# The last stage's value bias: added by a transfer from DRAM instead of by GpSimd, and a third hidden weight tile

## The reference, cut to what matters

```
def _L3_conv_ref(x, in_proj_weight, in_proj_bias, hid_proj_weight, hid_proj_bias, out_proj_weight, out_proj_bias):
    qkv = in_proj_weight[None] * x[:, None, :, :, :, None] + in_proj_bias[None]
    q = softplus(qkv[:, 0].reshape(n, -1, a))
    k = softplus(qkv[:, 1].reshape(n, -1, a))
    v = qkv[:, 2].reshape(n, -1, a)
    s = cumsum(k[:, :, :, None] * v[:, :, None, :], axis=1)
    z = cumsum(k, axis=1)
    y = einsum('nsi,nsij->nsj', q, s) / einsum('nsi,nsi->ns', q, z)[:, :, None]
    y = concatenate([ones_like(y[:, :1]), y[:, :-1]], axis=1)
    y = sum(hid_proj_weight[None] * y[:, None], axis=-1) + hid_proj_bias[None]
    y = sum(out_proj_weight[None] * tanh(y), axis=1) + out_proj_bias[None]
```

## Time and profile before

| what | us |
|---|---|
| median of three runs (3159.19, 3159.97, 3163.45) | 3159.97 |
| the profiled execution | 3161.46 |
| its span in the trace | 3159.7 |
| busy in it: VectorE | 1936.3 |
| GpSimd | 1770.5 |
| TensorE | 1537.9 |
| ScalarE | 863.4 |
| last stage, from about 2196 to the end | 964 |

### The profile page before, as it was taken

How to read it: one execution, slowest core, us unless ns; L and a number is a source line. 1 busy time by engine, 2 the same in 40 slices (tenths; PEclk the granted TensorE clock), 3 DMA queues, 4 the chain that set the end, 5 groups by cost and what they waited for, 6 DMA issues and landing times. The chain is left out here.

```text
span 3159.7 us, 31596 instructions
## 1 busy us (share of the span) xinstructions
PE 1537.9 (49%) x11604; PEld 875.4 (28%) x11604; DVE 1936.3 (61%) x1751; ACT 863.4 (27%) x1126; POOL 1770.5 (56%) x1350
## 2 busy tenths in 40 slices
PE   3656551323222222223222220054688888898998
PEld 2545420101000100001000010043255555555555
DVE  4222145555555545555455554467899999999995
ACT  2111151111111111111111110053545545455451
POOL 2000017777777777777777777605455465564652
PEclk9787865555555555555555555568799999999999
DMA  9999864655555445555555545233031231322312
GB/s 365 404 429 429 366 172 133 160 146 141 133 148 149 134 133 139 153 138 137 137 141 152 135 133 136 85 127 84 7 121 64 83 106 66 117 69 76 113 64 94
DMA packets 337029, 483.27 MB, mean 153 GB/s; under 512 B 185920, under 2 KB 277076, under 8 KB 319184
## 3 DMA queue, kind: packets, MB, share of 16 engines
q1 hardware_dynamic: 278256, 329.84, 30.8%
q0 software_dynamic: 58720, 152.72, 17.3%
HBM read 396.89 MB, written 85.45 MB: 153 GB/s over the span
## 5 line engine op out<-in xcount | busy, mean ns | idle before, releaser
L435 POOL DMA_INDIRECT gath<-table,idx x1152 | 1212.1, 1052 | 436.8 <-issue 375.3
L610 DVE TENSOR_TENSOR gath<-gath,p_stat 128x2304 f32<-128x2304 f32 x128 | 326.9, 2554 | 749.8 <-DMA gath<-table,idx 672.6
L647 PE MATMUL p_z<-wz,pairs 128*128 128x384 f32 x384 | 266.8, 827 | 456.0 <-issue 452.3
L493 ACT ACTIVATE zt<-p_z 128x384 f32<-128x384 f32 x192 | 93.5, 491 | 984.6 <-remote 627.2
L647 PEld LDWEIGHTS p_z<-wz,pairs 128*128 128x128 f32 x384 | 100.9, 302 | 610.6 <-issue 600.2
L637 PE MATMUL p_conv<-sides,wconv 128*128 128x512 f32 x64 | 66.2, 1138 | 398.7 <-issue 314.6
L1039 POOL TENSOR_TENSOR gated<-gated,outw_early 128x512 f32<-128x512 f32 x64 | 133.0, 2078 | 216.4 <-ACT gated L1100 216.4
L1269 PE MATMUL p_state<-xt,tri_early 128*128 128x512 f32 x512 | 235.2, 602 | 28.5 <-DVE prod L1155 28.5
L1155 DVE TENSOR_TENSOR prod<-p_state,query 128x2048 f32<-128x2048 f32 x80 | 182.0, 2275 | 54.4 <-PE p_state L1279 53.8
L289 PE MATMUL acc<-ring,win_a 128*32 128x128 f32 x3072 | 135.1, 342 | 145.2 <-DMA ring<-in_w 126.6
L655 PE MATMUL p_y<-ident,yt 128*128 128x128 f32 x64 | 17.8, 432 | 382.3 <-DVE yt L618 382.3
(11 more groups left out here) (242 smaller groups left out, 3084.4 us busy)
## 6 DMA issues: line engine op xcount, KB each, us to landing
ring<-in_w SPq DMA_DIRECT2D x64, 2304.0 KB, 19.4
hidw<-in_hidw SPq DMA_DIRECT2D x64, 1024.0 KB, 5.3
table<-zt SPq DMA_DIRECT2D x256, 144.0 KB
table<-zt SPq DMA_DIRECT2D x512, 72.0 KB
gath<-table,idx POOLq DMA_INDIRECT x1152
xt<-in_x SPq DMA_DIRECT2D x4, 1024.0 KB, 8.0
resid<-xt SPq DMA_DIRECT2D x32, 128.0 KB, 2.4
xlate<-resid SPq DMA_DIRECT2D x16, 256.0 KB, 2.8
```

The lines of the kernel that those rows point to most:

```text
L435: nc.gpsimd.indirect_dma_start(out=gath[:, t % SLOTS, k].rearrange("p n c -> p (n c)"), out_offset=None, in_=tables[u], in_offset=bass.Ind ...
L610: tt(g, g, w, ALU.mult).then_inc(weighted, 1)
L647: nc.tensor.matmul(p_z[i % ZS][:], pairs[u][:, 4 * J:4 * J + 4].rearrange("p j w -> p (j w)"), wz[:, m * WIDE:(m + 1) * WIDE], start=True, ...
```

## The change

Every bias of the value is now added by a transfer that GpSimd issues: it reads `inb_value` (1 MB) from DRAM and adds it to the tile `value` on chip (`accum_op=ALU.add`). It increments `v_ready` by 16 when it has landed, and VectorE waits for that in `keys_x_values`. GpSimd waits for the projection of the value before it issues, and goes on to the query's bias. The tile `inb` shrinks from 3 to 2 MB, and the megabyte holds a third tile for hidden weights. With `HOME = (0, 1, 2, 1)` block 0 and block 2 have tiles of their own and are loaded once. Blocks 1 and 3 share the second tile: block 3 is asked for after step 1, block 1 after step 3.

```
--- before.py
+++ after.py
@@ -890,7 +890,7 @@
 
 
 ATT = 4
-EARLY = {"inw": [P, 3 * ATT, HALF], "inb": [P, 3 * ATT, HALF], "tri": [P, P], "pick": [P, ATT + 1, 32], "give": [P, ATT + 1, P],
+EARLY = {"inw": [P, 3 * ATT, HALF], "inb": [P, 2 * ATT, HALF], "tri": [P, P], "pick": [P, ATT + 1, 32], "give": [P, ATT + 1, P],
          "outb": [P, HALF], "edge": [P, 2], "hidb": [P, ATT, HALF], "outw": [P, ATT, HALF]}
 
 
@@ -923,7 +923,8 @@
         key, value = sb("key", [P, A, HALF]), sb("value", [P, A, HALF])
         query = [sb(f"query{n}", [P, A, HALF]) for n in range(2)]
         expo, lift = sb("expo", [P, A, HALF]), sb("lift", [P, A, HALF])
-        hidw = [sb(f"hidw{n}", [P, A, HALF]) for n in range(2)]
+        hidw = [sb(f"hidw{n}", [P, A, HALF]) for n in range(3)]
+        HOME = (0, 1, 2, 1)
         prod = [sb(f"prod{n}", [P, A, HALF]) for n in range(2)]
         y = sb("y", [P, A, HALF]); gated = sb("gated", [P, A, HALF])
         xh = sb("xh", [P, HALF]); xlate = sb("xlate", [P, HALF])
@@ -949,7 +950,7 @@
         hidw_in = [sem(f"hidw_in{n}") for n in range(2)]
         xh_ready = sem("xh_ready"); x_turned = sem("x_turned")
         v_scaled = sem("v_scaled"); v_ready = sem("v_ready"); k_scaled = sem("k_scaled"); q_scaled = sem("q_scaled")
-        biased = sem("biased"); absd = sem("absd"); expd = sem("expd"); lifted = sem("lifted"); lost_ready = sem("lost_ready")
+        bias_begun = sem("bias_begun"); biased = sem("biased"); absd = sem("absd"); expd = sem("expd"); lifted = sem("lifted"); lost_ready = sem("lost_ready")
         logd = sem("logd"); rectified = sem("rectified"); eased = sem("eased"); soft = sem("soft")
         kv_ready = sem("kv_ready"); totalled = sem("totalled"); edge_zero = sem("edge_zero"); carry_ready = sem("carry_ready")
         state_ready = sem("state_ready"); queried = sem("queried"); summed = sem("summed")
@@ -980,12 +981,12 @@
                     sp.dma_start(xh[h * C:(h + 1) * C], rows[bass.ds(b, 1), h].rearrange("o c x -> (o c) x")).then_inc(x_in, 16)
 
             def hidden_weights(a):
-                sp.dma_start(hidw[a % 2][:], d["hidw"][:, a]).then_inc(hidw_in[a % 2], 16)
+                sp.dma_start(hidw[HOME[a]][:], d["hidw"][:, a]).then_inc(hidw_in[a % 2], 16)
 
             sp.wait_ge(x_turned, 1)
             load(1)
-            hidden_weights(0)
-            hidden_weights(1)
+            for a in (0, 2, 1):
+                hidden_weights(a)
 
             def main(b, u, left):
                 if left == 2:
@@ -999,7 +1000,7 @@
                     sp.wait_ge(o_ready, b)
                     sp.dma_start(slots[bass.ds(b - 1, 1)].rearrange("o m k p -> (o m) k p"),
                                  o[:].rearrange("m (k p) -> m k p", k=4)).then_inc(out_done, 16)
-                for a in range(A if left else A - 2):
+                for a in (1, 3) if left else (1,):
                     sp.wait_ge(hid_scaled, b * A + (a + 1))
                     hidden_weights((a + 2) % A)
 
@@ -1026,7 +1027,9 @@
 
             def inputs(b, u):
                 add_bias(key, 1, k_scaled, b, biased)
-                add_bias(value, 2, v_scaled, b, v_ready)
+                pool.wait_ge(v_scaled, b + 1)
+                pool.sem_inc(bias_begun, 1)
+                pool.dma_start(value[:], d["inb_value"][:], accum_op=ALU.add).then_inc(v_ready, 16)
                 add_bias(query[u], 0, q_scaled, b, biased)
                 take_lost(key, b, 0)
                 take_lost(query[u], b, 1)
@@ -1038,7 +1041,8 @@
                     pool.wait_ge(tanh_ready, b * A + (a + 1))
                     tt(gated[:, a], gated[:, a], outw[:, a], ALU.mult).then_inc(gated_ready, 1)
 
-            add_bias(value, 2, v_scaled, 0, v_ready)
+            pool.wait_ge(v_scaled, 1)
+            pool.dma_start(value[:], d["inb_value"][:], accum_op=ALU.add).then_inc(v_ready, 16)
             pool.wait_ge(eased, 1)
             take_lost(query[0], 0, 1, prod[0])
             over_batches(pool, main)
@@ -1135,7 +1139,7 @@
             def keys_x_values(b, j):
                 if j == 0:
                     dve.wait_ge(soft, b * 2 + 1)
-                    dve.wait_ge(v_ready, b + 1)
+                    dve.wait_ge(v_ready, b * 16 + 16)
                 tt(kv[:, j], key[:], value[:, j:j + 1].to_broadcast([P, A, HALF]), ALU.mult).then_inc(kv_ready, 1)
 
             def column_carries(b):
@@ -1173,8 +1177,11 @@
                     dve.wait_ge(summed, b * TERMS + (A + a))
                 else:
                     dve.wait_ge(hid_summed, b * A + (a - 1))
-                dve.wait_ge(hidw_in[a % 2], b * 32 + (a // 2 * 16 + 16))
-                tt(prod[(u + TERMS + a) % 2][:], hidw[a % 2][:], y[:], ALU.mult).then_inc(hid_scaled, 1)
+                if a % 2:
+                    dve.wait_ge(hidw_in[1], b * 32 + (a // 2 * 16 + 16))
+                elif known(b) and b == 0 and a == 0:
+                    dve.wait_ge(hidw_in[0], 32)
+                tt(prod[(u + TERMS + a) % 2][:], hidw[HOME[a]][:], y[:], ALU.mult).then_inc(hid_scaled, 1)
 
             def main(b, u, left):
                 times_query(b, u, 0)
@@ -1456,7 +1463,8 @@
         n = len(lead)
         return v.transpose((n + 1,) + tuple(range(n)) + (n + 3, n, n + 2))
     a["inw"] = by_token(f("L3_conv_in_proj_weight"), (3,), 0).reshape(P, 12, HALF)
-    a["inb"] = by_token(f("L3_conv_in_proj_bias"), (3,), 0).reshape(P, 12, HALF)
+    inb = by_token(f("L3_conv_in_proj_bias"), (3,), 0).reshape(P, 12, HALF)
+    a["inb"], a["inb_value"] = inb[:, 0:8], inb[:, 8:12]
     a["hidw"] = by_column(f("L3_conv_hid_proj_weight"), (4,), 1).reshape(P, 4, 4, HALF)
     a["hidb"] = by_column(f("L3_conv_hid_proj_bias"), (4,), 1).reshape(P, 4, HALF)
     a["outw"] = by_token(f("L3_conv_out_proj_weight"), (4,), 1).reshape(P, 4, HALF)
```

## The result

| | us |
|---|---|
| before, median of 10 runs (3159.19 to 3164.57) | 3162.31 |
| changed, median of 10 runs (3150.97 to 3155.74) | 3153.18 |
| ratio, with its 95% interval | 0.9974 [0.9966, 0.9982] |
| the profiled execution of the changed kernel | 3152.95 |
| its span | 3151.1 |

The change is 9.1 us faster; 8.9 were forecast. The time itself is 2.1 us above the forecast of 3151.1. The three runs shown at first had a median of 3159.97, and ten have 3162.31.

A forecast was written before the change was run, and what follows sets the result against it. VectorE was taken to set the pace. Gains of 3.5 + 1.8 + 0.5 + 1.9 + 1.2 = 8.9 us took the profiled 3161.5 to 3152.6, and 1.5 off toward the median gave 3151.1; range 3144 to 3160 us.

The forecast's parts named there:

- The transfer, steady batches: Last stage, each steady batch: issue and landing take 9.6 us, hidden while under 18.1, so 0 us.
- GpSimd's relief: Fifteen batches of the last stage: value bias off GpSimd saves VectorE 0.24 us before add_log, 3.5 us in all.
- Rival C: Steady batches: TensorE swallows the 0.24 us, leaving 5.4 us of gain and 3154.6 us; chance 0.10.
- the 0.42: Key's lost_part in steady batches: us given back when GpSimd's query bias no longer meets it; VectorE gains only 0.24.
- The start of the stage: Before batch 0: value ready at 2221.7, products start at 2221.8 instead of 2223.6, a gain of 1.8 us.
- the sum of 6.4: Total gain in us if the first transfer's issue waited for lost_part, the start losing 0.7 instead of gaining 1.8.
- The weights, middle batches: Hidden steps: most removed weight waits return as step 3 duration; gains 0.5 us in batch 13, 1.9 in batch 2.
- Rival B: Hidden steps: all 13.3 us of weight waits come back as gain, giving 3140.0 us; chance 0.08.
- The last batch: Last batch's hidden step 3: block 3 fetched alone lets it start earlier, a gain of 1.2 us.
- alone it lands 5.3 later: Last batch: block 3, asked for at 3142.17, lands at 3147.5, instead of step 3 starting at 3148.71.
- The total: Whole kernel: the terms sum to 8.9 us of gain, forecast 3151.1 us, chance 0.50.

The follow-up runs named there:

- the tile alone: Third weight tile and two weight loads a batch, GpSimd still adding to the value (query's bias as stand-in), against the kernel before: ratio 0.9997, 3044.35 us against 3044.72.
- the second profile: Changed kernel unaltered, timed and profiled again beside later runs, against the kernel before: ratio 0.9975, 3150.49 us against 3159.75.
- the transfer alone: Changed kernel with the two weight tiles and four weight loads a batch of before, against the kernel before: ratio 0.9979, 3040.11 us against 3044.72.
- the hold on GpSimd's product in both kernels: Second gated product held until hidden step 3 is done; against the kernel before (3159.75 us): changed kernel 3135.16 us, ratio 0.9922; kernel before 3148.84, ratio 0.9965.

## Why the prediction was right, point by point

**The transfer, steady batches.** Right. I took 9.6 us of issue and landing from two plain transfers and a second read. Measured (duration ns min/median/max, and us to landing):

```profile
L1032 POOL DMA_DIRECT2D value<-in_inb_value x15: 838/858/901, 2253.4 to 3044.3; - x15
L1045 POOL DMA_DIRECT2D value<-in_inb_value x1: 1015/1015/1015, 2212.3 to 2212.3; - x1
...
DMA to landing us min/median/max: 7.8/7.9/8.9
```

It lands after 7.9 us with the issue in it, inside the bounds and 1.7 under my value. A plain megabyte lands after 5.0 at the median with an issue of 0.34 in it, so the adding costs some 2.4 more behind the issue. The estimate from the Trainium skill's figures ("DMA: Bandwidth & Descriptors", Anatomy of one DMA, and "Collectives: The Full Stack", Part 3) is 6.8 for two source reads. With an issue of 0.9 it meets the 7.9 more closely than mine, and the trace agrees with it to 0.2 us; that the second read is what costs the 2.4 no run here shows.

**GpSimd's relief.** Right in kind and size: 0.24 us a steady batch, and 3.2 us from batch 0 to batch 15 against the tile alone, where 3.5 were forecast for the fifteen. Rival C would have needed the gain to vanish. TensorE does take the rest of the 0.42, as the prediction put it.

**The start of the stage.** Right in kind, too small in size: 1.8 forecast, 2.8 measured at the first `keys_x_values` and 3.4 at the first hidden step (2.6 in the second profile). The mis-sized term is the landing, 8.1 us here instead of 9.6. In the trace of the changed kernel:

```profile
2212.11 2.29 DVE L1132 SCALAR_TENSOR_TENSOR expo<-lift,expo 128x2048 f32<-128x2048 f32 x1 [0.41 <-ACT lift L1074]
2212.34 1.01 POOL L1045 DMA_DIRECT2D value<-in_inb_value  x1 [18.48 <-DVE value L1127]
...
2217.14 2.29 DVE L1137 TENSOR_TENSOR key<-key,lift 128x2048 f32<-128x2048 f32 x1 [0.33 <-ACT lift L1084]
...
2220.52 4.49 DVE L1143 TENSOR_TENSOR xt<-key,value 128x2048 f32<-128x2048 f32 x2 [1.09 <-DMA value<-in_inb_value]
```

`lost_part` takes 2.29 instead of 6.38, and the products start 26.8 us into the stage, 1.0 sooner than I had it (2221.8 is 27.7). The issue runs inside `lost_part`. It takes 1.01 us, 0.15 more than the median of the others, and `lost_part` isn't held up. The Trainium skill ("SBUF — State Buffer", Who interferes with whom) infers that a tensor_tensor, which takes only the read side of the port, doesn't starve the descriptors. `lost_part` is a scalar_tensor_tensor that reads two tiles on chip; for it the trace agrees, and the sum of 6.4 falls. (The section that the prediction names has the page's warning; the inference stands in this one.)

**The weights, middle batches.** Right. Wait plus duration of step 3 was 3.28, and is 3.26 with no wait. The gain is 1.8 at batch 2 and 0.5 at batch 13, against 1.9 and 0.5; I had missed 0.3 in batch 0. The places were those of one execution, though: with the transfer alone, on the same two tiles, the losses lay in other batches. Against that kernel the tile is worth 3.0. The third tile alone and the hold on GpSimd's product in both kernels show the mechanism: the waits came back only in part because GpSimd took the port in the meantime. Rival B falls.

**The last batch.** Wrong. The step that failed is "alone it lands 5.3 later". The issue and the step that waits for it:

```profile
3132.52 0.34 SPq L984 DMA_DIRECT2D hidw<-in_hidw  x1
...
3138.74 2.29 DVE L1184 TENSOR_TENSOR prod<-hidw,y 128x2048 f32<-128x2048 f32 x1 [4.04 <-DMA hidw<-in_hidw]
...
3141.09 2.48 PE L1320 MATMUL p_sum<-ident,prod 128*128 128x128 f32 x16 [3.94 <-DVE prod L1184]
```

It lands 6.1 us after the issue, nearly what it took before beside block 2 (6.4). Step 3 itself starts only 0.3 us nearer to step 0 than before, where the sum had 1.2. That holds in the second profile too (a landing of 6.2, and step 3 0.2 nearer).

The rest was TensorE's clock. Behind step 3, TensorE went to work after 3.94 us without any (the last of the rows), and 1.3 us later its granted clock fell to the lower of its two levels, 1.2 GHz of 2.4. In the second profile that stretch came earlier, behind 3.10 us without work. There it held up step 2 by 1.5 us, which cost nothing, since step 3 had to wait for its weights anyway. The granted clock is the third number from the end, first in the first profile, then in the second, with the matmuls that it slowed there (3.63 us where the same sixteen take 1.97 at full clock):

```profile
3142.40:3145.80 3.40, 3.40 (x12) 2.26 (x11) 0.00 (x0) 0.60 (x1) 1.26 (x1) 0.50 0.00 0
...
3129.60:3133.00 3.40, 3.40 (x17) 3.40 (x18) 2.03 (x1) 0.00 (x0) 0.00 (x0) 0.50 0.25 36
...
3129.49 3.63 PE L1320 MATMUL p_sum<-ident,prod 128*128 128x128 f32 x16 [3.10 <-DVE prod L1184]
```

From the end of step 3 to the end of the stage the second profile takes 8.4 us, and the first 10.1. All twelve profiles divide in this way: 8.4 to 8.5 in the seven whose clock is full behind step 3, the kernel before among them, and 9.6 to 11.0 in the five with a lower stretch there. So the end lost 1.1 in the first profile and gained 0.5 in the second, of 1.2 forecast. It is the least steady part: 21.3 to 23.9 us in the kernels here that fetch block 3 late, and 18.5 with the block fetched early.

Why the megabyte takes 6.1 here was not settled, but the traces have a trail. Of the loads of block 3 in the first profile of the changed kernel, the fourteen of batches 0 to 13 that run alone land after 4.8 to 5.2 us. The last two land after 6.2 and 6.1, and beside these the DMA profile shows one transfer of 0.02 MB on the queue for instructions. No run separates the two.

**The total.** 8.9 forecast, 9.1 measured in the medians, and 8.2 and 9.1 in the stage of the two profiles. Misses cancel, and in part that is luck. In the first profile the start and batch 0 gave 1.9 more than forecast, and the last batch 2.3 less; in the second the start and batch 0 gave 1.1 more and the last batch 0.7 less.

## What to carry to other kernels

When VectorE and GpSimd both read two tiles on chip, look at wait plus duration, not at the wait alone: a wait that is removed in front of such a port comes back as duration, and the table of waits overstates what can be had. Work taken from GpSimd pays at the point where it stood in front of a VectorE operation, which may be nowhere near the chain of waits. A transfer that adds is cheap for GpSimd, 0.9 us, as long as it is issued ahead of its need by the 7.8 to 8.9 us that it took here.

## What the hardware showed that I had not expected

GpSimd can win the port from back-to-back VectorE operations. Its second `gated` product had been pending during step 2 and got in before step 3 in every batch without a wait, although step 3 was ready at once. An operation of 1.3 us on GpSimd so costs VectorE 1.1, and a single added wait on GpSimd's side brought the changed kernel 15.3 us.

The three chips differ, far from the change. The stage of the deformable convolution, whose gathers GpSimd issues, in two kernels that are the same there (us, busy us per engine, clock, DMA share, GB/s), first the changed kernel in its second profile, then the kernel with the transfer alone, on another chip:

```profile
456.00:2043.00 1587.00, 373.69 (x528) 129.34 (x526) 834.12 (x838) 237.06 (x480) 1212.03 (x1152) 0.53 0.52 140
```

```profile
456.00:1932.00 1476.00, 271.43 (x526) 118.84 (x525) 825.94 (x834) 237.96 (x478) 1127.38 (x1144) 0.55 0.53 149
```

111 us of difference, with the layer before it equal and the one behind it within a microsecond (149 and 148). Each kernel of a group shows its group's level, with the kernel before at 3159.75, 3044.72 and 3045.38 us. Whether it is the chip itself or something that stayed the same for a group, such as where its data lay, no run here shows. Ratios have to be taken within a group.
